# Products without a reader between the stages of a sequential scan on TensorE

## The chip, the cores and the metric

One core of one Trainium2 chip runs the whole program. The metric is the device time of one execution in microseconds (us), median over several executions.

## What is computed

The reference is a small network of four parts. The first is a sequential one: for each of 4 rows a state of 512 values is carried through 512 time steps of a Runge-Kutta integration, four derivatives to a step, and each derivative holds a product of the tanh of the state with a 512x512 matrix:

```python
def _derivative(q, p, drive, coupling, bias):
    i_couple = jnp.tanh(q) @ coupling.T
    dq = q - q ** 3 / 3.0 - p + drive + i_couple + bias
    dp = EPSILON * (q + ALPHA - BETA * p)
    return (dq, dp)
...
x = x + _L0_attn_ref(_L0_cond_ref(cond_2048, cond_2048, x, ...), Wqkv_w, Wqkv_b)
x = x + _L0_ffn_ref(_L0_cond2_ref(x, cond_2048, ...), up_weight, ...)
```

Then come a causal attention over the 512 steps, a transformer block with a wide attention, and a feed-forward layer with signs for weights.

## The kernel before

`scan_phase` holds the part that the change touches. It does the 512 steps one after the other, each in 4 stages, so 2048 stages in a chain. The state lies as 128 partitions x (4 chunks x 4 rows). One stage goes around three engines:

- ScalarE takes the tanh of the state in two halves (L263, float16, and L264, float32). The first half signals `s_th`.
- VectorE forms what float16 left out (`low_part`, L533) and signals `s_tl`.
- TensorE (`one_step`) multiplies the 4x4 blocks of the matrix. First 16 products with the low part of the weights (`low_blocks`, L411, 4 columns each, waits on `s_th` per half), then 16 with the high part (`high_blocks`, L419, 8 columns each, waits on `s_tl` per half). Each product loads a 128x128 float16 weight of its own. After the first 8 and after all 16 high products it signals `s_mm`.
- VectorE adds the sums to the state with one scan instruction per half (L543), which signals `s_q`, for which ScalarE's next tanh waits. Between them VectorE does the elementwise work of the integration (L527 and others), and GpSimd (L662) some of it.

TensorE's own program order is: transposes of the inputs, then the steps. Most steps are in hardware loops of 2 steps (`plain`). Where later phases need something prepared, `one_step` takes a function `behind`, called after each stage's 32 products: `turn` (one transpose of 128 columns in each stage of the even steps 8 to 30), `ada_part` (one small float32 product in each stage of steps 32 to 55) and, from the second chunk of 64 steps on, `qk_product` and `v_product` (one product of 256 columns into `fill_bank`, L381 and L387, in 12 of the 16 stages of a group of 4 steps, 12 groups to a chunk; in the other 4 stages `behind` does nothing). After the steps TensorE does the last chunk's products in one go, and the program passes an all-engine barrier to the next phase. The PSUM of the scan is four `bank`s, `ada_bank` and `fill_bank`; the change takes a further bank.

Of the kernel before, what the change touches and what calls it, by code (L numbers as in the profile page):

```python
# [22 lines left out]
P = 128  # L23
# [7 lines left out]
STAGES = 4  # L31
UNROLL = 4
PE_UNROLL = 2
HALVES = (slice(0, C // 2), slice(C // 2, C))


# [30 lines left out]
ADA_AT, ADA_PER, ADA_SLOTS = 32, 3, 4  # L67
# [12 lines left out]
def scan_phase(nc, io, x_dram, u_dram, swapped_dram, v_dram, ada_dram):  # L80
    sems = []
    with ExitStack() as ctx:
        def sb(n, s, d): return ctx.enter_context(nc.sbuf_tensor(n, s, d))
        def ps(n): return ctx.enter_context(nc.psum_tensor(n, [P, 512], F32))
# [11 lines left out]
        w_hi = sb("w_hi", [P, 3, C, D], F16)  # L96
# [25 lines left out]
        factors = sb("factors", [P, 5, C, B], F32)  # L122
        p_sum = sb("p_sum", [P, C, B], F32)
        banks = [ps(f"bank{i}") for i in range(4)]
        ada_bank, fill_bank = ps("ada_bank"), ps("fill_bank")

        wq = wT[:, :, :, :].rearrange("p i c d -> p (i c d)").bitcast(F16).rearrange("p (a c n) -> p a c n", a=2, c=C)
        scaled = sb("scaled", [P, 2, D], F32)
# [113 lines left out]
        def _(act):  # L242
# [15 lines left out]
            def one_step(t, behind=None):  # L258
                for s in range(STAGES):
                    u = s % 2  # L260
                    for half, at in enumerate(HALVES):
                        act.wait_ge(s_q, t * 2 * STAGES + (2 * s + half + 1))
# [67 lines left out]
        def _(pe):  # L330
# [18 lines left out]
            for c in range(C):  # L349
                last = pe.matmul(banks[0][:, c * B:(c + 1) * B], cond_rows[:, c * P:(c + 1) * P], identity[0:B, 0:B],  # L350
                                 start=(c == 0), stop=(c == C - 1), skip_group_check=True)
# [4 lines left out]
            def ada_part(m, k):  # L356

                e = m // ADA_PER
                if m % ADA_PER == 0 and k == 0:
                    pe.wait_ge(s_ada_w[e % ADA_SLOTS], 16 * (e // ADA_SLOTS + 1))  # L360
                at = m % ADA_PER * P
                last = pe.matmul(ada_bank[:, m * B:(m + 1) * B], ada_w[e % ADA_SLOTS][:, k, at:at + P], condT[:, k, :],
                                 start=(m == 0 and k == 0), stop=(m == ADA - 1 and k == C - 1), skip_group_check=True)
                if k == C - 1:
                    last.then_inc(s_ada, 1)
# [23 lines left out]
            def behind(i, product, free):  # L389

                def of(s):
                    x = 4 * i + s
                    if x == 0:
                        pe.wait_ge(s_free, free)
                    if x < 12:
                        last = product(x)
                        if x == 11:
                            last.then_inc(s_group, 1)
                return of

            def one_step(t, behind=None):
                for s in range(STAGES):
                    u, w_of = s % 2, WEIGHTS_OF[s]
                    out = banks[2 * u:2 * u + 2]

                    def low_blocks(outputs, inputs):

                        for m in outputs:
                            sums = out[m // 2][:, (m % 2) * 3 * B:(m % 2 + 1) * 3 * B].rearrange("p (b n) -> p b n", n=3)
                            for k in inputs:  # L410
                                pe.matmul(sums[:, :, 2], w_lo[:, w_of, k, m * P:(m + 1) * P], tanh_parts[:, u, k, :, 0],  # L411
                                          start=(m % 2 == 0 and k == 0), stop=False, skip_group_check=True)

                    def high_blocks(outputs, inputs):

                        for m in outputs:
                            sums = out[m // 2][:, (m % 2) * 3 * B:(m % 2 + 1) * 3 * B].rearrange("p (b n) -> p b n", n=3)
                            for k in inputs:
                                last = pe.matmul(sums[:, :, 1:3], w_hi[:, w_of, k, m * P:(m + 1) * P], tanh_parts[:, u, k],  # L419
                                                 start=False, stop=(m % 2 == 1 and k == C - 1), skip_group_check=True)  # L420
                        return last

                    pe.wait_ge(s_th, t * 2 * STAGES + (2 * s + 1))
                    low_blocks((0, 1, 2, 3), (0, 1))
                    pe.wait_ge(s_th, t * 2 * STAGES + (2 * s + 2))
                    low_blocks((0, 1, 2, 3), (2, 3))
                    pe.wait_ge(s_tl, t * 2 * STAGES + (2 * s + 1))
                    high_blocks((0, 1), (0, 1))
                    pe.wait_ge(s_tl, t * 2 * STAGES + (2 * s + 2))
                    high_blocks((0, 1), (2, 3)).then_inc(s_mm, 1)  # L430
                    high_blocks((2, 3), (0, 1, 2, 3)).then_inc(s_mm, 1)
                    if behind is not None:
                        behind(s)

            def plain(first, count):
                with pe.Fori(0, count // PE_UNROLL) as steps:
                    for i in range(PE_UNROLL):
                        one_step(steps * PE_UNROLL + (i + first))

            plain(0, TURN_AT)  # L440
            for t in range(TURN_AT, ADA_AT):
                m, odd = (t - TURN_AT) // 2, (t - TURN_AT) % 2
                one_step(t, None if odd else lambda s: turn(m, s))
            for m in range(ADA):
                one_step(ADA_AT + m, lambda s: ada_part(m, s))
            plain(ADA_AT + ADA, CHUNK - ADA_AT - ADA)
            pe.wait_ge(s_wlo, 2 * WT)
            for c in range(1, CHUNKS):
                at, free = c * CHUNK, FREE_TURNS + GROUPS0 * (c - 1)
# [6 lines left out]
                at, free = at + 8 * C, free + 2 * C  # L456
# [9 lines left out]
            for j in range(GROUPS0):  # L466
                if j >= 4:
                    pe.wait_ge(s_free, FREE_TURNS + GROUPS0 * (CHUNKS - 1) + j - 3)
                for x in range(12):
                    if j == 0 and x % 3 == 0:  # L470
                        pe.wait_ge(s_tail, x // 3 + 1)
                    if j < 2 * C:
                        m = j // 2 + j % 2 * C
# [7 lines left out]
        def _(v):  # L481
# [47 lines left out]
            def low_part(t, s, half):  # L529

                u, at = s % 2, HALVES[half]
                v.wait_ge(s_tf, t * 2 * STAGES + (2 * s + half + 1))
# [3 lines left out]
            def result(t, s, between=None):  # L536

                u, to = s % 2, (s + 1) % STAGES
                for half, at in enumerate(HALVES):
                    v.wait_ge(s_mm, t * 2 * STAGES + (2 * s + half + 1))  # L540
# [213 lines left out]
def product(pe, out, weight, activation, chunks):  # L754

    n = 0
    for k in range(chunks):
        for a, b in PRODUCTS:
            last = pe.matmul(out, weight(a, k), activation(b, k), start=(n == 0), stop=(n == 3 * chunks - 1))  # L759
            n += 1  # L760
    return last
# [1474 lines left out]
def program(nc, io, out):  # L2236
    def dram(name, dt=F32): return nc.dram_tensor(name, (P, C, B, T), dt, kind="Internal").ap()
    x_dram, xa_dram, x3_base, x3_dram = [dram(n) for n in ("x_t", "xa_t", "x3b_t", "x3_t")]
    u_dram, swapped_dram = [nc.dram_tensor(n, (P, 2 * C * B, T), F32, kind="Internal").ap() for n in ("u_t", "swapped_t")]
    v_dram = nc.dram_tensor("v_t", (B, T, D), F32, kind="Internal").ap()  # L2240
    n1 = [dram(f"n1_{p}") for p in PARTS]
    n2 = [dram(f"n2_{p}") for p in PARTS]
    ada_dram = nc.dram_tensor("ada_t", (P, ADA, B), F32, kind="Internal").ap()
    scan_phase(nc, io, x_dram, u_dram, swapped_dram, v_dram, ada_dram)
    causal_phase(nc, io, x_dram, u_dram, swapped_dram, v_dram, xa_dram)
    attention_phase(nc, io, xa_dram, ada_dram, n1, n2, x3_base)
    ffn_phase(nc, io, False, n2, ada_dram, x3_base, x3_dram)
    ffn_phase(nc, io, True, [x3_dram], None, xa_dram, out)
# [15 lines left out]
```

## Time and profile before

| | |
|---|---|
| median of 3 runs | 5296.73 us (5296.2 to 5300.87) |
| the profiled execution: its own time | 5296.68 us |
| its span, first to last instruction | 5294.9 us |
| mean granted TensorE clock | 0.701 |
| busy: PE, PE loads, DVE, ACT, POOL | 85%, 71%, 79%, 43%, 33% |
| the scan's steps, about 47.5 to 2907 us | 2859.5 us |

PE is TensorE's matmul, PEld its weight load, DVE is VectorE, ACT ScalarE, POOL GpSimd. The granted clock is given as a share of TensorE's full 2.4 GHz; 0.50 is its low level, 1.2 GHz. Busy shares are averages over phases with different limits, so the text works with stretches. Matmuls are pipelined: a record of 170 ns does not keep the next one from starting 27 ns later.

### The profile page before, as it was taken

The page shows a single profiled execution, that of the slowest core. Times are in us where ns is not written, and L with a number is a line of the kernel's source. Part 1 is how long each engine was busy: PE and PEld are TensorE (multiplying, and loading weights), DVE is VectorE, ACT ScalarE, POOL GpSimd, SP SyncE. Part 2 cuts the span into 40 slices and gives each one's busy share as a digit, 9 for nine tenths or more (in the row PEclk, how much of TensorE's full clock was granted, in tenths as well). Part 3 has the DMA queues.
Part 4 walks back from the last instruction along what each step waited for, and adds up shares of the span by engine and source line. Part 5 has one row for each costly group of instructions (what it writes and reads, how often), then busy time and mean ns, then how long its engine had stood idle before and what let it go on. Part 6 is the DMA issues. An engine that isn't in the chain of part 4 may idle for free. (4 is left out here: it accounts for less than half of the span.)

```text
span 5294.9 us, 213524 instructions
## 1 busy us (share of the span) xinstructions
PE 4524.0 (85%) x79177; PEld 3744.4 (71%) x79177; DVE 4172.0 (79%) x25401; ACT 2299.9 (43%) x10591; POOL 1725.2 (33%) x6044
## 2 busy tenths in 40 slices
PE   6898878878888788788787576899999999789899
PEld 5796666666666666666666465687777787568787
DVE  8999999999999999999999587677777777621123
ACT  4434433334334333343343565555555555432243
POOL 2444444444444444444443332232333222100000
PEclk5555555555555555555555788899999999899999
DMA  3000010010100100100001321222222222140221
GB/s 111 20 21 2 1 23 1 2 22 1 18 7 1 23 1 2 22 1 11 14 1 23 109 101 59 79 76 84 69 95 72 82 70 76 38 146 32 70 74 40
DMA packets 228443, 225.44 MB, mean 43 GB/s; under 512 B 81612, under 2 KB 151700, under 8 KB 227640
## 3 DMA queue, kind: packets, MB, share of 16 engines
q1 hardware_dynamic: 226416, 216.25, 13.5%
q8 instruction: 345, 5.65, 0.4%
q14 instruction: 330, 2.70, 0.2%
q0 software_dynamic: 448, 0.69, 0.1%
q10 hardware_dynamic: 904, 0.15, 0.0%
HBM read 160.37 MB, written 56.67 MB: 41 GB/s over the span
## 5 line engine op out<-in xcount | busy, mean ns | idle before, releaser
L411 PEld LDWEIGHTS bank<-tanh_parts,w_lo 128*128 128x128 f16 x32768 | 1037.6, 105 | 836.0 <-ACT tanh_parts L263 806.6
L263 ACT ACTIVATE tanh_parts<-ys 128x8 f16<-128x8 f32 x4096 | 858.9, 210 | 1735.9 <-DVE ys L543 1735.9
L411 PE MATMUL bank<-tanh_parts,w_lo 128*128 128x4 f16 x32768 | 1211.4, 169 | 447.5 <-ACT tanh_parts L263 305.3
L419 PE MATMUL bank<-tanh_parts,w_hi 128*128 128x8 f16 x32768 | 1180.0, 173 | 24.2 <-DVE tanh_parts L533 17.0
L419 PEld LDWEIGHTS bank<-tanh_parts,w_hi 128*128 128x128 f16 x32768 | 1037.3, 104 | 31.3 <-DVE tanh_parts L533 21.6
L543 DVE TENSOR_TENSOR_SCAN ys<-mix,bank 128x24 f32<-128x24 f32 x4096 | 823.9, 203 | 101.1 <-PE bank L419 33.7
L264 ACT ACTIVATE tanh_full<-ys 128x8 f32<-128x8 f32 x4096 | 804.6, 196 | 0.0
L533 DVE TENSOR_TENSOR tanh_parts<-tanh_full,tanh_parts 128x8 f16<-128x8 f32 x4096 | 646.3, 164 | 1.6 <-ACT tanh_full L264 1.1
L1383 POOL TENSOR_TENSOR t_w_qk<-t_raw_qk,t_w_qk 128x512 fp32r<-128x512 f32 x128 | 168.2, 1336 | 683.6 <-ACT t_w_qk L1547 683.6
L759 PE MATMUL t_bank<-t_x,t_w_qk 128*128 128x512 f32 x1536 | 361.5, 391 | 12.8 <-DVE t_x L1803 12.8
L759 PEld LDWEIGHTS t_bank<-t_x,t_w_qk 128*128 128x128 f32 x1536 | 290.1, 189 | 74.0 <-DVE t_x L1803 13.5
L527 DVE SCALAR_TENSOR_TENSOR cub<-ys 128x16 f32<-128x16 f32 x1536 | 305.2, 199 | 0.0
L1579 ACT ACTIVATE t_probs<-t_scores,t_shift 128x512 f32<-128x512 f32 x256 | 174.0, 688 | 256.6 <-DVE t_shift L1742 256.4
L527 DVE SCALAR_TENSOR_TENSOR rate<-p_stages,ys 128x16 f32<-128x16 f32 x1536 | 270.2, 176 | 17.7
L527 DVE SCALAR_TENSOR_TENSOR slope<-cub,ys 128x16 f32<-128x16 f32 x1536 | 264.2, 172 | 0.0
L662 POOL TENSOR_TENSOR gq<-q,factors 128x16 f32<-128x16 f32 x512 | 114.1, 223 | 449.6 <-DVE rate L527 449.6
L527 DVE SCALAR_TENSOR_TENSOR p_stages<-rate,p 128x16 f32<-128x16 f32 x1536 | 256.7, 167 | 0.0
L2172 DVE TENSOR_TENSOR g_h<-g_h 128x512 fp32r<-128x512 f32 x64 | 44.3, 692 | 267.1 <-ACT g_h L2150 267.1
L381 PE MATMUL fill_bank<-states,wT 128*128 128x256 f16 x672 | 251.3, 374 | 0.0
L662 POOL TENSOR_TENSOR gp<-rate 128x16 f32<-128x16 f32 x512 | 129.8, 253 | 336.0 <-DVE rate L527 336.0
L1475 PE MATMUL t_scores<-t_k,t_q 128*128 128x512 f32 x768 | 204.4, 402 | 35.5 <-ACT t_probs L1579 24.4
L662 POOL TENSOR_TENSOR gp<-rate,factors 128x16 f32<-128x16 f32 x512 | 113.9, 222 | 361.3 <-DVE rate L527 361.3
(210 smaller groups left out, 9271.4 us busy)
## 6 DMA issues: line engine op xcount, KB each, us to landing
t_raw_qk<-L_cond_qkv_w_dram SPq DMA_DIRECT2D x128, 256.0 KB, 3.2
t_raw_vo<-L_cond_qkv_w_dram SPq DMA_DIRECT2D x16, 1024.0 KB, 5.1
t_raw_vo<-L_cond_out_w_dram SPq DMA_DIRECT2D x16, 1024.0 KB, 5.1
n<-t_parts SPq DMA_DIRECT2D x14, 1024.0 KB, 6.6
u_t<-u_out SPq DMA_DIRECT2D x32, 256.0 KB, 2.7
swapped_t<-u_out SPq DMA_DIRECT2D x256, 32.0 KB, 1.9
u<-u_t SPq DMA_DIRECT2D x32, 256.0 KB, 2.6
swapped<-swapped_t SPq DMA_DIRECT2D x32, 256.0 KB, 2.9
```

The costliest lines, as they stand in the source:

```text
L263: act.activation(tanh_parts[:, u, at, :, 0], ys[:, s, at, :, 2], ACT.Tanh, scale=1.0 / SCALE).then_inc(s_th, 1)
L264: act.activation(tanh_full[:, u, at], ys[:, s, at, :, 2], ACT.Tanh, scale=1.0 / SCALE).then_inc(s_tf, 1)
L381: return pe.matmul(bank[:, 0:B * CHUNK], wq[:, a, k, m], states[:, b, k, :], start=(x == 0), stop=(x == 11))
L411: pe.matmul(sums[:, :, 2], w_lo[:, w_of, k, m * P:(m + 1) * P], tanh_parts[:, u, k, :, 0], start=(m % 2 == 0 and k == 0), stop=False, skip ...
L419: last = pe.matmul(sums[:, :, 1:3], w_hi[:, w_of, k, m * P:(m + 1) * P], tanh_parts[:, u, k], start=False, stop=(m % 2 == 1 and k == C - 1 ...
L527: return v.scalar_tensor_tensor(out=out, in0=in0, scalar=scalar, in1=in1, op0=op0, op1=op1)
L533: v.tensor_tensor(tanh_parts[:, u, at, :, 1], tanh_full[:, u, at], tanh_parts[:, u, at, :, 0], ALU.subtract).then_inc(s_tl, 1)
L543: v.tensor_tensor_scan(ys[:, to, at].rearrange("p c b n -> p (c b n)"), mix[:, at].rearrange("p c b n -> p (c b n)"), banks[2 * u + half][ ...
L662: return g.tensor_tensor(out, a, b, op)
L759: last = pe.matmul(out, weight(a, k), activation(b, k), start=(n == 0), stop=(n == 3 * chunks - 1))
L1475: last = pe.matmul(score_bank[i % 2][:, :], q_p[a][:, i * P:(i + 1) * P], k_p[b][:, :], start=(n == 0), stop=(n == 2))
L1579: act.activation(probs[:, i, :], score_bank[i % 2][:, :], ACT.Exp, bias=shift[:, i:i + 1], scale=SCORE_SCALE, accum_out=sums[:, i:i + 1]). ...
```

## The change

`idle_products(columns)` issues matmuls of at most 512 columns into a bank that nobody reads, with weights and data from `w_hi`. It stands at the end of each stage, behind `behind`: 1024 columns where the step has no `behind`, 768 where it has one, and 1024 in the steps of `ada_part`. Before the first step stand 16 products of 512 columns. No wait and no signal is added, and no other engine's program changes.

```diff
+IDLE_COLUMNS, BEHIND_COLUMNS = 1024, 256
...
-        ada_bank, fill_bank = ps("ada_bank"), ps("fill_bank")
+        ada_bank, fill_bank, idle_bank = ps("ada_bank"), ps("fill_bank"), ps("idle_bank")
...
-            def one_step(t, behind=None):
+            def idle_products(columns):
+                for at in range(0, columns, 512):
+                    wide = min(512, columns - at)
+                    pe.matmul(idle_bank[:, 0:wide], w_hi[:, 0, 0, 0:P], w_hi[:, 0, 1, 0:wide], start=True, stop=True)
+
+            def one_step(t, behind=None, taken=BEHIND_COLUMNS):
...
                     if behind is not None:
                         behind(s)
+                    idle_products(IDLE_COLUMNS if behind is None else IDLE_COLUMNS - taken)
...
+            idle_products(16 * 512)
             plain(0, TURN_AT)
...
-                one_step(ADA_AT + m, lambda s: ada_part(m, s))
+                one_step(ADA_AT + m, lambda s: ada_part(m, s), 0)
```

## Rows read from the trace of the kernel before

**Rows 1.** The page: span, busy share, and 40 slices of it with the clock.

```profile
span 5294.9 us, 213524 instructions
PEclk5555555555555555555555788899999999899999
```

**Rows 2.** Stretch of all steps: busy us (count) by engine, clock, DMA share, GB/s.

```profile
47.50:2907.00 2859.50, 2389.89 (x66752) 1994.48 (x66752) 2722.19 (x23029) 1123.58 (x8346) 1211.23 (x5711) 0.50 0.06 13
```

**Rows 3.** Timeline of one stage and the next one's start: start, us, engine, work.

```profile
1200.80 0.21 ACT L263 ACTIVATE tanh_parts<-ys 128x8 f16<-128x8 f32 x1 [0.84 <-DVE ys L543]
...
1201.07 0.50 PEld L411 LDWEIGHTS bank<-tanh_parts,w_lo 128*128 128x128 f16 x16 [0.41 <-ACT tanh_parts L263]
...
1201.49 0.50 PEld L419 LDWEIGHTS bank<-tanh_parts,w_hi 128*128 128x128 f16 x16
1201.52 0.57 PE L419 MATMUL bank<-tanh_parts,w_hi 128*128 128x8 f16 x16
...
1201.80 0.18 DVE L527 SCALAR_TENSOR_TENSOR p_stages<-rate,p 128x16 f32<-128x16 f32 x1
...
1201.92 0.20 DVE L543 TENSOR_TENSOR_SCAN ys<-mix,bank 128x24 f32<-128x24 f32 x1
...
1202.15 0.21 ACT L263 ACTIVATE tanh_parts<-ys 128x8 f16<-128x8 f32 x1 [0.83 <-DVE ys L543]
...
1202.42 0.51 PEld L411 LDWEIGHTS bank<-tanh_parts,w_lo 128*128 128x128 f16 x16 [0.39 <-ACT tanh_parts L263]
```

**Rows 4.** The same a step later, first stage's low products.

```profile
1206.24 0.21 ACT L263 ACTIVATE tanh_parts<-ys 128x8 f16<-128x8 f32 x1 [0.84 <-DVE ys L543]
```

**Rows 5.** Groups of TensorE's products in the stretch of all steps.

```profile
L411 PE MATMUL bank<-tanh_parts,w_lo 128*128 128x4 f16 x32752 | 1210.8, 169 | 447.2 <-ACT tanh_parts L263 304.9 <-issue 27.5
L419 PE MATMUL bank<-tanh_parts,w_hi 128*128 128x8 f16 x32752 | 1179.4, 173 | 24.2 <-DVE tanh_parts L533 17.0 <-issue 5.9
L381 PE MATMUL fill_bank<-states,wT 128*128 128x256 f16 x672 | 251.3, 374 | 0.0
L362 PE MATMUL ada_bank<-condT,xT 128*128 128x4 f32 x192 | 54.5, 354 | 0.0
```

**Rows 6.** Stretch of four stages with a 256-column product in each.

```profile
1659.50:1664.90 5.40, 4.95 (x136) 3.78 (x134) 5.20 (x47) 2.10 (x16) 2.27 (x11) 0.50 0.00 2
```

**Rows 7.** Timeline and stretches of two bursts of 512-column products, low clock.

```profile
3308.58 3.75 PE L1427 MATMUL t_bank<-t_parts,t_mean_w 128*128 128x512 f32 x8 [0.68 <-DVE t_parts L1764]
3317.29 4.76 PE L1427 MATMUL t_bank<-t_parts,t_mean_w 128*128 128x512 f32 x8 [4.96 <-DVE t_parts L1773]
...
3312.90:3316.30 3.40, 0.00 (x0) 0.00 (x0) 2.85 (x9) 1.05 (x2) 0.00 (x0) 1.00 0.60 183
3317.30:3322.10 4.80, 4.75 (x8) 1.99 (x8) 2.09 (x4) 4.72 (x7) 0.17 (x1) 0.50 0.00 0
```

**Rows 8.** Timeline and stretches around a gap, high clock before.

```profile
4122.19 3.01 PE L1453 MATMUL t_bank<-t_w_vo,t_x 128*128 128x512 f32 x12
4127.21 1.72 PE L1475 MATMUL t_scores<-t_k,t_q 128*128 128x512 f32 x6 [2.01 <-ACT t_probs L1579]
...
4125.20:4128.60 3.40, 1.39 (x6) 1.12 (x7) 3.33 (x7) 1.94 (x5) 0.00 (x0) 1.00 0.24 70
4128.70:4132.00 3.30, 3.30 (x9) 2.63 (x8) 3.20 (x8) 0.39 (x1) 0.00 (x0) 0.50 0.00 0
```

**Rows 9.** Stretch of attention rounds, no product over 256 columns.

```profile
3145.70:3155.80 10.10, 6.87 (x120) 5.92 (x117) 9.23 (x22) 7.84 (x19) 5.08 (x4) 1.00 0.75 252
```

**Rows 10.** Timeline of weight loads of 33-column products at the high clock, 24 in all.

```profile
3087.47 0.10 PEld L1000 LDWEIGHTS m_out<-val_hi,pt_hi 128*128 128x128 f16 x1
...
3088.06 0.10 PEld L1000 LDWEIGHTS m_out<-val_hi,pt_lo 128*128 128x128 f16 x1
```

**Rows 11.** What TensorE's loads waited for, 100 to 2900 us: us, times, longest.

```profile
PEld bank L411 <- ACT tanh_parts L263: 787.4, 1903, 0.5
PEld bank L411 <- issue: 28.0, 9, 4.3
```

**Rows 12.** Timeline: a wait that ends with issue, at a loop's end.

```profile
678.84 0.50 PEld L419 LDWEIGHTS bank<-tanh_parts,w_hi 128*128 128x128 f16 x16
682.79 0.51 PEld L411 LDWEIGHTS bank<-tanh_parts,w_lo 128*128 128x128 f16 x16 [3.44 <-issue]
```

**Rows 13.** Timeline of the head: the state is written, the first load starts.

```profile
46.07 0.17 DVE L507 TENSOR_SCALAR ys<-condT 128x16 f32<-128x16 f32 x1
...
47.58 0.51 PEld L411 LDWEIGHTS bank<-tanh_parts,w_lo 128*128 128x128 f16 x16 [2.13 <-ACT tanh_parts L263]
```

## The prediction

> **What bounds the kernel now.** I read the page first. The steps take 2859.5 of 5294.9 us, TensorE has the low clock in all of them (0.50, which is 1.2 GHz) and mostly the high one afterwards [rows 1, 2]. Next came the timeline of one stage, the unit that repeats 2048 times. In it the tanh of the first half starts at 1200.80, TensorE's first load at 1201.07, the high products at 1201.52. The eighth of them starts 7 spacings later; a row of 16 loads lasts 0.50 us with 0.10 us for one, so a spacing is 26.7 ns, and it ends at 1201.52 + 0.187 + 0.173 = 1201.88. VectorE's scan follows at 1201.92 and the next tanh at 1202.15 [rows 3, 5, 10]. So the chain is tanh, 24 pairs of load and product, scan. From this first load to the next is 1.35 us; over a whole step the tanh goes from 1200.80 to 1206.24, so 1.36 us a stage [rows 3, 4]. 2048 x 1.36 = 2785 us; the other 75 us of the 2859.5 are waits outside this pattern, among them nine "issue" waits of up to 4.3 us, 28.0 us in sum [rows 2, 11, 12].
>
> The reader should see two numbers beside the chain. TensorE's loads of a stage end at about 1201.89 (1201.49 + 15 x 0.0267) and the next begin at 1202.42: TensorE has 0.53 us in which it can take work for nothing, and it does wait for the tanh 1903 times [rows 3, 11]. And VectorE is nearly full: 2722 of 2859.5 us [rows 2].
>
> **The change part by part.** It removes nothing; it adds some 1.75 million columns, and moves nothing.
>
> *Price of the added columns at the low clock.* A 256-column product lasts 374 ns and an 8-column one 173: 201 / 248 = 0.81 ns a column, close to the 0.833 of 1.2 GHz [rows 5]. 1024 columns take 0.853 us. Only 0.53 us are free, so at the low clock TensorE itself becomes the bound: 32 x 26.7 ns + 0.853 us = 1.707 us a stage in place of 1.36. In that state all inputs lie ready 0.35 us before TensorE comes to them.
>
> *Price at the high clock.* Twelve 512-column products take 3.01 us, 0.24 each with the last one's drain [rows 8]. Two take 0.45 to 0.48 us and fit, just, in the 0.53 us. What stands to be won is then the chain's TensorE part. Its 24 pairs are spaced by loads: at the high clock 24 loads of the same shape go from 3087.47 to 3088.06, 25.7 ns each [rows 10] against 26.7. The first 8 low products gain nothing, since the ninth waits for the second tanh half. So the other 16 give 16 to 27 ns, and the shorter passage of the last product some 5 ns: about 30 ns a stage. VectorE sets the upper bound: p_stages at 1201.80 keeps it from the scan until about 1201.89, so this stage can win 30 ns at most, others by the same reading up to 70, 55 on average [rows 3]. The lower bound is 0, if the ready tanh and VectorE's parts come just behind. So 0 to 113 us over 2048 stages, and I take 60.
>
> The Trainium skill ("TensorE: Matmul & The Clock Gate", Back-to-back issue gap) says that start-to-start of small products never drops below about 25 ns at either clock. By it the clock's doubling is worth only 1.7 ns a pair, and not half of 26.7; the trace agrees with its 25.7. The same sum by halved pairs would be 24 x 13.3 = 320 ns a stage, which VectorE would stop at 55.
>
> So everything hangs on which clock is granted. *Does it stay high?* The 16 products at the head run back to back for several us; eight such in 3.75 us were followed by a stretch at 1.00 [rows 7], so I expect the first steps at the high clock. In it a stage is some 1.33 us and holds 1024 idle columns and 192 of its own (16 x 4 + 16 x 8). The nearest row for sparse 512-column work at the high clock: six products in the 3.4 us from 4125.2, after which the clock was 0.50 although it had been high and TensorE had been full before [rows 8]. In 3.4 us the changed scan has 5 such products on average, and its small ones. Against it stands the attention stretch with 120 products, none over 256 columns, TensorE busy 68%, at 1.00 throughout [rows 9]. Between these two the small products decide: whether 32 pairs with 6 columns on average weigh like their columns or like their time.
>
> *Does it come back when it has fallen?* At the low clock the changed scan has two 512-column products in 1.707 us, or eight in 6.8 us. Eight in 4.76 us stayed at 0.50; eight in 3.75 us did not [rows 7]. So the idle products alone do not bring it back, and again the pairs must. What the pairs weigh is bounded by the stages that already have a 256-column product: TensorE busy 4.95 of 5.40 us, clock 0.50 [rows 6]. Pairs take 0.85 of 1.36 us there and the fill 0.21, together 78%, and the clock did not rise. So pairs weigh less than their time. I take the value nearer to their columns, as the six sparse products do not weigh more than theirs either, and expect the fall, and no return. Even with a clock that holds in the quiet pattern, a wait like that from 679 to 683 us [rows 12] leaves TensorE without work for longer than the 2.01 us gap after which it fell in [rows 8].
>
> *The sum at the low clock.* 2048 x 1.707 = 3496 us. The stages whose `behind` does nothing have 768 columns: 7 chunks x 12 groups x 4 = 336 stages, less 256 columns each: -72. The 96 stages of `ada_part` hold 192 float32 records of about 0.2 us spacing each beside 1024 columns: +38. In `turn`'s 48 stages a float32 transpose of 128 columns takes the place of the 256: 0. Of the 75 us outside the pattern some 15 are late work of GpSimd that TensorE's backlog now hides; the issue waits stay: +60. In all 3522 against 2859.5: +662 us. The head: TensorE is free at about 46.3 and was needed at 47.58 [rows 13]. Some 8 products at 0.427 us and 8 at 0.24 take 5.3 us: +4. Nothing behind the steps changes; those phases begin after a barrier. The profiled execution's own time is 5296.68, the median of the runs 5296.73, so the same base: 5297 + 662 + 4 = 5963; with a little of the high clock at the start **5960 us**.
>
> **The rivals.**
> *Low from soon after the head (my forecast):* 5960, within 5880 to 5990 (bounds: the pattern's stalls hidden or not, and the first steps high or not). Chance 0.53.
> *High until one of the long issue waits, low after it:* if the first that counts is that at 679 us, 113 steps or 452 stages run at 1.33 and not 1.707, -170: 5790. For it: the pairs may weigh enough to hold, not enough to return. Chance 0.12.
> *High nearly throughout (the other side):* the pairs weigh at least about half of their time, so that at the low clock, where TensorE never rests, it returns within a few us after each wait. Then -60, +4 for the head, +14 for ten falls of about four stages at 0.35 us: 5255, within 5225 to 5285. It decides from the point where a stage of 32 pairs and 1024 columns is enough activity at 1.707 us. For it: TensorE would be busy without pause, and [rows 9]; against it: [rows 6, 8]. Chance 0.30. The Trainium skill (same page, Part 1: The HAM clock gate) says that the ratio is set by how busy TensorE has been recently, and its table advises to keep it busy continuously; taken by busy time, that rule gives this case. The trace does not agree by busy time: 0.50 at 4.95 of 5.40 us [rows 6].
> *No difference:* the high clock holds, but the idle products end just behind the next tanh and eat the 30 ns. Chance 0.05.
>
> **How the numbers follow.** About 0.2% (11 us) is what a measurement of this kernel can tell from no change. Slower is 0.53 + 0.12 = 0.65, faster 0.30, same 0.05. The two cases of most weight lie 700 us apart and hold 0.83; leaving the faster one out would leave out 3 in 10, so the range goes from 5225 to 5990. The likeliest case's own range is 5880 to 5990.
>
> **What would show it.** Right: the clock at 0.50 in all slices of the scan but the first, a load-to-load distance of 1.7 us between stages, TensorE waiting for no tanh, 512-column products of about 0.58 us, and ScalarE and VectorE with more idle time each stage. Wrong: 1.00 in the slices of the scan, stages of 1.33 us, short falls at issue waits. The prediction fails at one step: what the small pairs weigh for the clock. If they weigh enough, all 662 us are gone and the sign turns.

## The result, and the profile after

The changed kernel takes 5940.55 us (median of 4 runs, 5933.74 to 5943.36) against 5297.36 before: a ratio of 1.121, 95% interval 1.119 to 1.123. It is slower by 643 us; 5960 was forecast. The profiled execution spans 5940.4 us, 645.5 more than before.

The page of the changed kernel: the span, two lines of the slices, and the groups of TensorE's products in the scan and of the tanh. Behind it, the tanh's group on the page of the kernel before.

```profile
span 5940.4 us, 221748 instructions
...
PE   7999999999999999999999996769999999969989
...
PEclk5555555555555555555555557879999999979999
...
L419 PEld LDWEIGHTS bank<-tanh_parts,w_lo 128*128 128x128 f16 x32768 | 1340.0, 109 | 901.7 <-ACT tanh_parts L266 644.2
L407 PE MATMUL idle_bank<-w_hi 128*128 128x512 f16 (+1 forms) x4112 | 1833.2, 550 | 0.8 <-DVE bank L515 0.8
L266 ACT ACTIVATE tanh_parts<-ys 128x8 f16<-128x8 f32 x4096 | 866.8, 212 | 2375.7 <-DVE ys L553 2375.7
...
L419 PE MATMUL bank<-tanh_parts,w_lo 128*128 128x4 f16 x32768 | 1258.7, 171 | 26.4 <-issue 26.4
L427 PE MATMUL bank<-tanh_parts,w_hi 128*128 128x8 f16 x32768 | 1175.0, 173 | 5.2 <-issue 5.2
```

```profile
L263 ACT ACTIVATE tanh_parts<-ys 128x8 f16<-128x8 f32 x4096 | 858.9, 210 | 1735.9 <-DVE ys L543 1735.9
```

The reader should see a TensorE that hardly rests and still has the low clock. Before, the matmul side waited for the tanh [rows 5]; now its only idle time in front of the small products is 26.4 + 5.2 us of "issue", which is idle time for which the profile shows nothing that was waited for, and ScalarE waits 2375.7 us instead of 1735.9. (The weight loads still show a wait for the tanh. In the trace the first load of a stage starts while the last idle product still streams, at 59.34 us where the stage's first product starts at 59.67, so this wait costs nothing.)

Stretches of the changed kernel, in the columns of [rows 2]: the scan, its first microseconds, and the rest of it.

```profile
47.50:3553.00 3505.50, 3473.86 (x70861) 2529.66 (x70860) 2743.02 (x23030) 1129.79 (x8348) 1208.94 (x5712) 0.50 0.05 11
...
50.30:57.10 6.80, 6.21 (x120) 3.90 (x118) 3.94 (x36) 1.56 (x12) 1.28 (x6) 1.00 0.88 312
57.20:3553.00 3495.80, 3464.85 (x70735) 2524.88 (x70736) 2738.22 (x22987) 1127.47 (x8330) 1206.42 (x5700) 0.50 0.05 10
```

Its timeline from the head on, TensorE alone.

```profile
47.37 5.04 PE L407 MATMUL idle_bank<-w_hi 128*128 128x512 f16 x16 [0.76 <-DVE bank L515]
52.24 0.55 PE L419 MATMUL bank<-tanh_parts,w_lo 128*128 128x4 f16 x16
...
53.53 0.56 PE L419 MATMUL bank<-tanh_parts,w_lo 128*128 128x4 f16 x16
...
54.84 0.56 PE L419 MATMUL bank<-tanh_parts,w_lo 128*128 128x4 f16 x16
...
58.20 0.37 PE L419 MATMUL bank<-tanh_parts,w_lo 128*128 128x4 f16 x8 [1.69 <-issue]
58.44 0.57 PE L427 MATMUL bank<-tanh_parts,w_hi 128*128 128x8 f16 x16
58.86 1.01 PE L407 MATMUL idle_bank<-w_hi 128*128 128x512 f16 x2
59.67 0.61 PE L419 MATMUL bank<-tanh_parts,w_lo 128*128 128x4 f16 x16
...
61.38 0.61 PE L419 MATMUL bank<-tanh_parts,w_lo 128*128 128x4 f16 x16
```

The 16 products at the head take 5.04 us and bring the clock up; from 52.24 to 53.53 and to 54.84 a stage takes 1.29 and 1.31 us. An issue wait of 1.69 us follows, the clock is down from 57.1, inside that wait, and from 59.67 to 61.38 a stage takes 1.71 us. It stays so for 3496 us.

One table will be used below. It is worked out from the starts of the first-half tanh in each trace: the median distance from one stage to the next, by the stage that it begins with and by the clock.

| kernel | clock | stage 0 | stage 1 | stage 2 | stage 3 |
|---|---|---|---|---|---|
| before | low | 1363 ns | 1353 | 1354 | 1378 |
| changed | low | 1706 | 1706 | 1706 | 1706 |
| changed, with bursts | high | 1366 | 1318 | 1313 | 1375 |
| all small products wide, no idle ones | high | 1385 | 1384 | 1385 | 1385 |
| small products partly wide, 1024 idle columns | high | 1366 | 1322 | 1313 | 1375 |
| before, VectorE's order changed | low | 1434 | 1400 | 1354 | 1467 |
| partly wide, order changed | high | 1435 | 1385 | 1313 | 1458 |

### The profile page after: what moved, and what is told of

It is laid out like the page before. It is cut to its first block and busy times, and to the rows that moved or that the text cites. A ratio compares the mean times of both kernels' runs of the same rounds, so it can differ in the third digit from the quotient of the medians.

```text
span 5940.4 us, 221748 instructions
## 1 busy us (share of the span) xinstructions
PE 5610.8 (94%) x83289; PEld 4281.7 (72%) x83289; DVE 4193.3 (71%) x25401; ACT 2304.7 (39%) x10591; POOL 1722.1 (29%) x6044
## 5 line engine op out<-in xcount | busy, mean ns | idle before, releaser
L419 PEld LDWEIGHTS bank<-tanh_parts,w_lo 128*128 128x128 f16 x32768 | 1340.0, 109 | 901.7 <-ACT tanh_parts L266 644.2
L407 PE MATMUL idle_bank<-w_hi 128*128 128x512 f16 (+1 forms) x4112 | 1833.2, 550 | 0.8 <-DVE bank L515 0.8
L266 ACT ACTIVATE tanh_parts<-ys 128x8 f16<-128x8 f32 x4096 | 866.8, 212 | 2375.7 <-DVE ys L553 2375.7
L419 PE MATMUL bank<-tanh_parts,w_lo 128*128 128x4 f16 x32768 | 1258.7, 171 | 26.4 <-issue 26.4
L543 DVE TENSOR_TENSOR tanh_parts<-tanh_full,tanh_parts 128x8 f16<-128x8 f32 x4096 | 683.2, 167 | 0.5 <-ACT tanh_full L267 0.5
L407 PEld LDWEIGHTS idle_bank<-w_hi 128*128 128x128 f16 x4112 | 422.5, 121 | 69.8 <-issue 1.9
L537 DVE SCALAR_TENSOR_TENSOR cub<-ys 128x16 f32<-128x16 f32 x1536 | 288.7, 188 | 0.0
L672 POOL TENSOR_TENSOR net<-drive_now,p 128x16 f32<-128x16 f32 x512 | 113.2, 221 | 526.8 <-DVE p L640 526.7
```

The lines of the kernel that those rows point to most:

```text
L266: act.activation(tanh_parts[:, u, at, :, 0], ys[:, s, at, :, 2], ACT.Tanh, scale=1.0 / SCALE).then_inc(s_th, 1)
L407: pe.matmul(idle_bank[:, 0:wide], w_hi[:, 0, 0, 0:P], w_hi[:, 0, 1, 0:wide], start=True, stop=True)
L537: return v.scalar_tensor_tensor(out=out, in0=in0, scalar=scalar, in1=in1, op0=op0, op1=op1)
L543: v.tensor_tensor(tanh_parts[:, u, at, :, 1], tanh_full[:, u, at], tanh_parts[:, u, at, :, 0], ALU.subtract).then_inc(s_tl, 1)
L672: return g.tensor_tensor(out, a, b, op)
```

## The experiments

**1. One idle product instead of two.** The 16 at the head stay.

```diff
-IDLE_COLUMNS, BEHIND_COLUMNS = 1024, 256
+IDLE_COLUMNS, BEHIND_COLUMNS = 512, 256
...
-                one_step(ADA_AT + m, lambda s: ada_part(m, s), 0)
+                one_step(ADA_AT + m, lambda s: ada_part(m, s), 512)
```

> One product of 512 columns behind each stage in place of two (256 where other work stands, none in the steps of ada_part); the 16 at the head stay. My theory (the loss is what 1024 columns overrun of the 0.53 us gap at the low clock): 512 columns take 0.427 us there, they fit, a stage stays at 1.36 us, clock 0.50, time before plus 4 us for the head: 5297 to 5305. Rival (the added products cost by themselves, through PSUM, the queue or fetching more instructions): half of the products, half of the loss, about 5620.

5304.77 us, ratio 1.0012 (1.0003 to 1.0022); clock 0.50 in the scan after the head. Half of the columns cost not half of the 643 us but 6. In the profiled executions the first small product starts 1.9 us later than before, and the issue waits in the scan add up to 37 us instead of 30. So it is not the products as such (their writes to PSUM, their place in the queue, their fetching) that costs the 643 us, but what sticks out of the gap.

**2. No head.** The changed kernel without `idle_products(16 * 512)` ahead of the steps.

> The changed kernel without the 16 products at its head. My theory (the head costs 4 to 5 us and buys four stages at the high clock, 2 us): 5936 to 5941, the scan at 0.50 from its first stage. Rival (the state at the head decides for the whole scan): it can only be slower or the same; no gain either way.

5941.67 us (5938.21 to 5944.56), ratio to before 1.1215 (1.1198 to 1.1232), as the changed kernel; the clock is 0.50 from the first step to the last. The head neither makes nor mends the loss.

**3. Bursts.** Does the clock fall by itself, or only at issue waits? The changed kernel gets 16 products at 21 more places.

```diff
             for c in range(1, CHUNKS):
...
+                idle_products(16 * 512)
                 plain(at, SPLIT_STEPS)
...
                 pe.wait_ge(s_split, C * c)
+                idle_products(16 * 512)
...
                 at += 16
+                idle_products(16 * 512)
```

> The changed kernel with 16 products of 512 columns more at three places of each of the 7 later chunks, outside the hardware loops. Theory A (the clock falls in the quiet pattern of the stages itself): after each burst it is high for a few stages only, 5940 plus 21 bursts of about 5 us, some 6030. Theory B (only an issue wait brings it down, and then it does not return): high from each burst to the next issue wait, that is most of the seven chunks at 1.31 us a stage; 5350 to 5500.

5971.07 us (one run). Stretches of it between bursts, and its timeline around one fall.

```profile
1355.60:1386.10 30.50, 30.50 (x744) 20.92 (x743) 26.91 (x236) 10.93 (x84) 11.39 (x55) 1.00 0.42 73
1386.30:1406.60 20.30, 20.30 (x358) 12.35 (x355) 14.59 (x124) 5.81 (x44) 7.17 (x34) 0.50 0.00 1
1406.80:1423.70 16.90, 16.77 (x381) 11.38 (x380) 13.59 (x116) 5.30 (x40) 5.83 (x27) 1.00 0.01 3
1423.90:1461.20 37.30, 37.30 (x719) 23.88 (x717) 30.53 (x244) 11.62 (x88) 15.42 (x66) 0.50 0.00 1
...
1478.50:1785.50 307.00, 301.26 (x6303) 227.94 (x6300) 241.52 (x2045) 100.36 (x740) 103.85 (x504) 0.50 0.01 3
```

```profile
1420.76 0.59 PE L407 MATMUL idle_bank<-w_hi 128*128 128x512 f16 x2
...
1422.46 0.59 PE L407 MATMUL idle_bank<-w_hi 128*128 128x512 f16 x2
...
1423.77 1.01 PE L407 MATMUL idle_bank<-w_hi 128*128 128x512 f16 x2
1424.58 0.61 PE L419 MATMUL bank<-tanh_parts,w_lo 128*128 128x4 f16 x16
```

Each of the 21 bursts brought the clock up, for 4 to 22 stages. In the 7.5 us before a fall the longest distance between two starts of matmuls was 0.22 to 0.43 us, so no issue wait was there: the quiet pattern with 1024 idle columns does not hold the high clock. And over the 307 us without a burst, TensorE busy 98% of the time, it did not come back. That is theory A. Its time was 6030 and 5971 were measured: the roughly 160 stages at the high clock that the bursts bought, some 0.36 us shorter each, give back about 60 us, of which the expectation took off little.

**4. More idle products.** 1536 and 2048 columns behind each stage in place of 1024.

> Three products of 512 columns behind each stage (1280 columns where other work stands, 1536 in the steps of ada_part), between 1024, which does not hold the high clock, and 2048, which does. If the clock is high in most of the scan: a stage of 0.80 + 0.65 = 1.45 us, 5297 + 2048 x 0.09 = 5480 to 5500. If it falls at an issue wait and does not return: 0.85 + 1.28 = 2.13 us, up to 6850. Since 2048 columns return in some windows only, I expect that 1536 hold the high clock in the quiet pattern and do not return well: a mixed trace, 5600 to 6850.

> Four products of 512 columns behind each stage in place of two (1792 columns where other work stands, 2048 in the steps of ada_part). My theory (TensorE is the bound by what it executes, and the clock goes by how much it streams): at the low clock a stage would be 0.85 + 1.71 = 2.56 us, at the high one 0.80 + 0.87 = 1.67 us. Two thirds of the low-clock stage are streaming, between the changed kernel's half, which does not return, and back-to-back work, which does; I expect a mixed or high clock, and 5950 (high) to 7750 (low). Rival (the gate gives the high clock to any TensorE without a pause): it would have returned in the changed kernel already, and here too.

5485.24 and 5888.73 us (one run each), clock 1.00 in both nearly throughout. Stretches around an issue wait with 1536 columns, then with 2048.

```profile
78.90:741.00 662.10, 657.24 (x15586) 517.21 (x15584) 589.25 (x4893) 247.97 (x1823) 268.16 (x1231) 1.00 0.04 10
741.10:751.20 10.10, 4.57 (x76) 3.16 (x77) 2.78 (x26) 1.06 (x8) 0.73 (x4) 0.50 0.02 5
751.30:1119.90 368.60, 365.32 (x9039) 290.25 (x9036) 338.15 (x2854) 136.22 (x1028) 150.43 (x709) 1.00 0.05 9
```

```profile
51.20:822.50 771.30, 769.25 (x16494) 575.64 (x16492) 605.38 (x5040) 256.25 (x1875) 273.66 (x1264) 1.00 0.06 17
822.60:836.10 13.50, 9.41 (x145) 6.12 (x146) 4.66 (x39) 2.02 (x16) 1.50 (x7) 0.50 0.02 4
836.20:1256.00 419.80, 416.37 (x9222) 314.46 (x9221) 337.30 (x2841) 136.65 (x1021) 148.26 (x705) 1.00 0.04 8
```

With more products the kernel is faster than with two, since the clock falls at issue waits only (8 and 7 times, each within some us of two products that start 1.6 to 4.5 us apart) and is back after 3 to 14 us. My expectation that 1536 columns would return badly was wrong, and with 2048 the time lies 61 us under the 5950 that I had as the lower end; the 336 stages that have 256 columns less are about 36 of them. A stage is 1453 ns with 1536 columns and 1669 with 2048, so at the high clock too the products stick out, and neither beats the kernel before. In the short low stretches a stage is 2133 and 2560 ns, 427 more for each further product over the 1706 of two: the sum of the prediction holds there as well.

**5. Activity without idle products.** The small products stream 32 columns each: the operand is repeated, into columns of the same bank that nobody reads. Once with 512 idle columns, once with none.

```diff
-                                pe.matmul(sums[:, :, 2], w_lo[...], tanh_parts[:, u, k, :, 0],
+                                pe.matmul(sums[:, :, :, 2], w_lo[...],
+                                          tanh_parts[:, u, k, :, 0].unsqueeze(1).to_broadcast([P, LOW_TIMES, B]),
...
-                                last = pe.matmul(sums[:, :, 1:3], w_hi[...], tanh_parts[:, u, k],
+                                last = pe.matmul(sums[:, :, :, 1:3], w_hi[...],
+                                                 tanh_parts[:, u, k].unsqueeze(1).to_broadcast([P, HIGH_TIMES, B, 2]),
```

> As the one before, and each of the 32 small products of a stage streams 32 columns instead of 4 or 8: its operand is repeated, and the repeats go to columns of the same bank that nobody reads. At the low clock a pair is spaced by 26.7 ns, the time of 32 columns, so the repeats should cost nothing. My theory (the clock goes by columns streamed, not by time with pairs in flight): the clock is 1.00 in nearly the whole scan, comes back after each issue wait, a stage is 1.31 us as in the changed kernel's first stages, time 5190 to 5230. Rival (clock indifferent to that, or pairs slow down with 32 columns): clock 0.50, 5300 or slower.

> The small products with 32 columns as before, no idle product behind the stages, the 16 at the head stay. My theory: 1024 columns in 1.36 us are as few as in the two idle products alone, the clock falls soon and stays at 0.50; a stage stays at 1.36, 5297 to 5310, which also shows that repeating the operand costs nothing. Rival (the small products weigh more than columns once they are wide): clock 1.00, about 5200.

5354.32 us, ratio 1.0105 (1.0088 to 1.0122), and 5341.93, ratio 1.0085 (1.0068 to 1.0101). Two surprises. The clock was 1.00 even without any idle product, so the forecast that it would fall there was wrong. And the repeats are not free: 5190 to 5230 were expected with 512 idle columns, from stages of 1.31 us. The timeline of one stage of the kernel without idle products:

```profile
1200.96 0.64 PE L424 MATMUL bank<-tanh_parts,w_lo 128*128 128x32 f16 x16 [0.23 <-ACT tanh_parts L267]
1201.41 0.48 PEld L433 LDWEIGHTS bank<-tanh_parts,w_hi 128*128 128x128 f16 x16
1201.44 0.56 PE L433 MATMUL bank<-tanh_parts,w_hi 128*128 128x32 f16 x16
```

Starts of wide low products lie 29 ns apart at the high clock and 53 at the low one (medians), wide high products 25 and 40; the narrow ones 25 and 27. A wide low product lasts 193 ns, a narrow one 166. That lengthens the chain: a stage is 1385 ns, and in all four stages the scan starts 0.04 us after the end of the eighth high product.

**6. Wide only where nobody waits.** Repeats of four, in the first 8 low products (the ninth waits for the second tanh half) and in 14 of the 16 high ones, the last ahead of each signal narrow; 1024 idle columns, 512 in the steps of `ada_part`. And the same with 512 idle columns.

```diff
+                                times = LOW_TIMES if k < 2 else 1
...
+                                times = 1 if m % 2 == 1 and k == C - 1 else HIGH_TIMES
```

> The changed kernel (512 idle columns in the steps of ada_part), and of the small products those stream repeats whose length nobody waits for: the first 8 low ones 16 columns, 14 of the 16 high ones 32; the last one before each signal stays narrow, and the other 8 low ones too. My theory: the clock is 1.00 in nearly the whole scan and returns after each issue wait, a stage is 1.31 us as the changed kernel's first ones, 53 ns less than 1.36: 5297 - 108 + 5 for the head + 10 for the returns, some 5205 (5190 to 5230). Rival (VectorE or the second tanh half holds the stage at 1.36 to 1.38 whatever the clock, as with all products wide): 5300 to 5350.

> As the one before with 512 idle columns behind a stage (256 where other work stands, none in ada_part). With all products wide even no idle product held the clock. My theory: also 1.00 and 1.31 us a stage, 5190 to 5230, since 1024 columns fit the gap at the high clock as well. Rival (the narrow low products take away what held it): clock 0.50 or mixed, 5300 to 5500, since the wide products cost 40 ns each at the low clock.

With 1024: 5275.74 us (five runs), ratio 0.9958 (0.9944 to 0.9972). This version beats both kernels, the one before by 22 us and not by 92; it lies between my theory and the rival. With 512: 5317.53, ratio 1.0033 (1.0020 to 1.0045), as the rival had it and not my theory. Its clock was down for 427 us of the scan, in 51 stretches; the longest, 150 us, covers the steps of `ada_part`, where no idle product stands, and most of the others have no issue wait ahead of them. So these partly wide products do not hold the high clock throughout without the second idle product. In the profiled execution of the version with 1024, which took 5297, the clock was down once for 65 us, inside the steps of `ada_part`, where 512 idle columns stand; the other four executions (5273.58 to 5277.73, mean clock 0.966 to 0.967 against 0.959) probably did not have this stretch:

```profile
67.60:282.50 214.90, 205.53 (x5121) 154.92 (x5117) 205.92 (x1664) 92.15 (x641) 99.58 (x431) 1.00 0.10 30
282.70:347.40 64.70, 64.70 (x1205) 55.32 (x1202) 46.42 (x387) 21.15 (x136) 19.79 (x95) 0.50 0.09 27
347.50:699.00 351.50, 345.59 (x8878) 258.74 (x8875) 335.30 (x2889) 141.27 (x1062) 152.07 (x716) 1.00 0.01 2
```

The table says where the rest is: at the high clock stages 1 and 2 are 31 and 41 ns shorter than before, stages 0 and 3 hardly at all.

**7. VectorE's order.** Do stages 0 and 3 hang on VectorE? The instruction that forms the scan's addend (`mix`) goes ahead of `rate` in stage 0 and ahead of `p_new` in stage 3, once at the high clock (version of 6 with 1024) and once at the low one (kernel before).

```diff
-                stt(rate[:, 0], p[:, :, :], -BETA, q[:, :, :]).then_inc(s_rate, 1)
                 after("slope")
                 own("base", stt(mix[:, :, :, 1], net[:, :, :], H, slope[:, :, :]))
+                stt(rate[:, 0], p[:, :, :], -BETA, q[:, :, :]).then_inc(s_rate, 1)
...
+                after("slope")
+                own("base", v.tensor_tensor(mix[:, :, :, 1], slope[:, :, :], known[:, 3], ALU.add))
                 v.wait_ge(s_psum, t + 1)
                 own("moved", stt(p_new[:, :, :], rate[:, 3], EPSILON * H / 3, p_sum[:, :, :]))
-                after("slope")
-                own("base", v.tensor_tensor(mix[:, :, :, 1], slope[:, :, :], known[:, 3], ALU.add))
```

> The kernel with partly widened small products and 1024 idle columns, and two changes of order on VectorE: in stage 0 the instruction that forms the scan's addend goes ahead of the one that forms rate, in stage 3 ahead of the one that forms p_new. My theory (at the high clock stages 0 and 3 are held at 1.366 and 1.375 us by VectorE's order, which is why the clock was worth 20 ns a stage and not 30 to 53): both go to about 1.32 us, 512 x (0.045 + 0.055) = 51 us less than without, 5275 - 51 = 5224 (5210 to 5245). Rival (the same two stages are held by something else, GpSimd or the tanh): no change, 5275.

> The kernel before with the same two changes of order alone, clock 0.50. My theory: TensorE's pairs at the low clock hold stages 0 and 3 too, just behind VectorE, so the order is worth only 1363 and 1378 down to about 1353 ns, 512 x 0.035 = 18 us, 5279 (5270 to 5290). Rival (VectorE's order was all of it): as much as at the high clock, 5245.

5384.82 us, ratio to before 1.0165 (1.0151 to 1.0178), and 5399.64, ratio 1.0192 (1.0178 to 1.0206): 109 us slower than the version of experiment 6, and 103 slower than the kernel before, where 51 and 18 less were expected. VectorE in stage 0 of the kernel before, then of the same with the order changed:

```profile
1200.08 0.17 DVE L527 SCALAR_TENSOR_TENSOR slope<-cub,q 128x16 f32<-128x16 f32 x1
1200.17 0.17 DVE L527 SCALAR_TENSOR_TENSOR rate<-p,q 128x16 f32<-128x16 f32 x1
1200.28 0.18 DVE L527 SCALAR_TENSOR_TENSOR mix<-net,slope 128x16 f32<-128x16 f32 x1
1200.57 0.20 DVE L543 TENSOR_TENSOR_SCAN ys<-mix,bank 128x24 f32<-128x24 f32 x1
```

```profile
1205.10 0.17 DVE L527 SCALAR_TENSOR_TENSOR slope<-cub,q 128x16 f32<-128x16 f32 x1
1205.38 0.18 DVE L527 SCALAR_TENSOR_TENSOR mix<-net,slope 128x16 f32<-128x16 f32 x1
1205.47 0.17 DVE L527 SCALAR_TENSOR_TENSOR rate<-p,q 128x16 f32<-128x16 f32 x1
1205.66 0.20 DVE L543 TENSOR_TENSOR_SCAN ys<-mix,bank 128x24 f32<-128x24 f32 x1
```

`mix` follows `slope`, of which it needs the result, after 0.28 us in the changed order, and after 0.20 with `rate` between; from `mix` to the scan are 0.28 to 0.29 us in both. So in stage 0 the order makes the chain slope, mix, scan longer and not shorter. In stage 3 it is something else. Before, then with the order changed:

```profile
1204.15 0.17 DVE L527 SCALAR_TENSOR_TENSOR slope<-cub,ys 128x16 f32<-128x16 f32 x1
1204.24 0.17 DVE L527 SCALAR_TENSOR_TENSOR p_new<-rate,p_sum 128x16 f32<-128x16 f32 x1
1204.36 0.18 DVE L628 TENSOR_TENSOR mix<-slope,known 128x16 f32<-128x16 f32 x1
1204.45 0.17 DVE L630 TENSOR_SCALAR p<-p_new 128x16 f32<-128x16 f32 x1
```

```profile
1203.64 0.17 DVE L527 SCALAR_TENSOR_TENSOR slope<-cub,ys 128x16 f32<-128x16 f32 x1
1203.85 0.18 DVE L626 TENSOR_TENSOR mix<-slope,known 128x16 f32<-128x16 f32 x1
1203.94 0.17 DVE L527 SCALAR_TENSOR_TENSOR p_new<-rate,p_sum 128x16 f32<-128x16 f32 x1
1204.15 0.17 DVE L630 TENSOR_SCALAR p<-p_new 128x16 f32<-128x16 f32 x1
1204.23 0.30 DVE L543 TENSOR_TENSOR_SCAN ys<-mix,bank 128x24 f32<-128x24 f32 x2
```

`mix` starts 0.21 us after `slope` in both, so nothing is won by having it first; but `p`, which also stands ahead of the scan, now starts 0.51 us after `slope` instead of 0.30, and the scan has to wait behind it. Stage 1 became longer too (1353 to 1400 ns at the low clock, 1322 to 1385 at the high one), and stage 2 stayed as it was.

With this order stage 0 takes 1434 ns at the low clock and 1435 at the high one, stage 3 1467 and 1458, while stage 2, which was not touched, takes 1354 and 1313. For the order before, the traces answer the question too. The median distance from the end of the eighth high product to the scan is 37 ns in stages 1 and 2 at both clocks: there the scan starts as soon as TensorE is done. In stage 0 it is 47 ns at the low clock and 89 at the high one, in stage 3 61 and 69, while `mix` to the scan stays at 283 to 285 ns in these two stages. TensorE is done earlier at the high clock and the scan does not follow: stages 0 and 3 go by VectorE's chain whatever TensorE's clock.

## Why the prediction was right

**The overrun at the low clock.** 1.707 us forecast, 1706 ns measured. Experiment 1 shows that the gap decides. (The prediction reads the gap as 0.53 us, from the start of the last load; by its own spacing, 1.36 less 32 x 26.7 ns, it is 0.51. The sum did not use it.) The 336 stages whose `behind` does nothing take 1493 ns and those of `ada_part` 2133, by their starts in the trace. In the time, 3522 us were forecast for the steps and they took 3500.5 (from first to last tanh 3505.2, less 4.7 for the head). The mis-sized term is the +60 for waits outside the pattern. 2048 x 1.706 less 72, plus 96 x 0.427 for `ada_part`, is 3463; so 37 are left, of which 32 are the issue waits (26.4 + 5.2 on the page). TensorE's backlog hid nearly all of the other waits, not 15 us of them. This term is nearly all of the 20 us between 5960 and the time measured.

**The head.** +4 forecast; the first small product starts at 52.24 where 47.58 was the first load before, 4.7 us.

**The clock.** The forecast was a fall soon after the head and no return, and that is what the slices show. The first fall came with an issue wait, the case that I had as a further reason; experiment 3 shows that the pattern falls without one as well, 21 times of 21. The rival with a fall only at a long wait has no place then. The rival with a high clock throughout needed the clock to return at a stage of 32 pairs and 1024 columns; it did not in 3496 us. Which clock it would be was a choice of 0.53 against 0.30 on rows that point both ways, and the stated range held both signs. So the time at the low clock was worked out, but that the forecast has the right sign owes something to luck. The Trainium skill ("TensorE: Matmul & The Clock Gate", Part 1: The HAM clock gate) ties the ratio to how busy TensorE has been recently. Taken by the busy time of the profile, the trace does not agree: TensorE was busy 3465 of 3496 us at 0.50, with idle products in half of it.

**What the high clock is worth.** 30 ns a stage were taken, with 0 to 55 as bounds. Measured (before against the bursts' high stretches): -3, 35, 41 and 3 ns for the stages 0 to 3, 19 on average. The step that was off is the one on VectorE. It read its slack from stage 1 alone ("others by the same reading up to 70, 55 on average"), and the slack was measured to the instruction that stands ahead of the scan and not to the result that the scan waits for. In stage 0 `mix` starts at 1200.28 and the scan at 1200.57, 0.29 us later, and the median is 283 ns at both clocks. That did not bear on the forecast, which lay at the low clock; it would have halved the gain of the rival: about 40 us less 18.

The pairs' spacing was right: 25 ns at the high clock, 27 at the low one (medians over the scan). The floor of about 25 ns in the Trainium skill (same page, Back-to-back issue gap) agrees with it.

**What stays open.** What decides the granted clock was not settled. 1024 contiguous idle columns with narrow small products do not hold it high; wide, repeated small products do, without any idle one. The second pattern differs from the first in more than one thing: its columns lie in all 32 products, they are repeats, and the low products start further apart (29 ns instead of 25). No run separates these.

## What to carry to other kernels

Work added to keep TensorE's clock up has to be sized at the low clock, where it takes twice as long: what does not fit into the gap there is paid in full, and it is paid exactly when the clock has fallen. First read from a stretch at the high clock what the clock is worth for this chain; here spacing by weight loads went from 27 to 25 ns and the neighbour engine held half of the stages, so some 40 us stood against 660. If activity is wanted, it was cheaper here inside instructions for which nobody waits than behind them: with the repeats of experiment 6 and 1024 idle columns the clock held nearly throughout and a stage took 1313 to 1375 ns; with a third idle product instead it held too, and a stage took 1453.

## What was not expected of the hardware

Small products with a repeated, strided operand of 32 columns start 53 ns apart at the low clock (40 for the one with pairs of neighbours), against 27 with 4 or 8 columns; at the high clock 29 and 25. Whether the repeat or the stride does it was not tested. On VectorE, `mix` of stage 0 started 0.28 us after `slope` when it stood right behind it, and 0.20 us after it with `rate` between. That is no rule for dependent neighbours: `mix` of stage 3 stood right behind `slope` in the same run and started 0.21 us after it. In stage 0 the program has one more wait (for `net`, long fulfilled) between the two; whether that costs the 0.08 us was not tested. More idle products made the scan faster: 2048 columns 5889 us, 1536 5485, 1024 5941.
